# A two-layer convolution attention kernel: image 0's projections in free PSUM banks, and another table of slots

## What is computed

```python
h = _group_norm(x, gn_w, gn_b).reshape(B, C, H * W)
qkv = jnp.einsum('oc,bcn->bon', qkv_w, h) + qkv_b[None, :, None]
q, k, v = jnp.split(qkv, 3, axis=1)
attn = jax.nn.softmax(jnp.einsum('bcn,bcm->bnm', q, k) * scale, axis=-1)
h = jnp.einsum('bcm,bnm->bcn', v, attn)
x = x + (jnp.einsum('oc,bcn->bon', proj_w, h) + proj_b[None, :, None]).reshape(B, C, H, W)
...
q, k, v = (W x + b for (W, b) in ((Wq, bq), (Wk, bk), (Wv, bv)))
attn = jax.nn.softmax(jnp.einsum('bdi,bdj->bij', q, k), axis=-1)
x = gamma[0] * jnp.einsum('bcj,bij->bci', v, attn) + x
```

## Time and profile before

| | |
|---|---|
| median of 3 runs | 1599.27 us (1598.35 to 1600.09) |
| the profiled execution | 1598.83 us |
| its span, first to last instruction | 1597.1 us |
| PE / PEld busy | 1507.5 (94%) / 1095.0 (69%) us |
| DVE / ACT / POOL busy | 1289.0 (81%) / 1205.5 (75%) / 1245.6 (78%) us |
| mean granted TensorE clock | 0.997 |

### The profile page before, as it was taken

One profiled execution on the slowest core, in us unless ns is written; L12 is line 12 of the kernel. 1 busy time (PEld: TensorE's weight loads), 2 busy tenths in 40 slices (PEclk: granted clock), 3 DMA queues, 4 the chain that ended last, 5 costly groups with the idle time before them and its releaser, 6 DMA issues. The chain is left out here.

```text
span 1597.1 us, 43928 instructions
## 1 busy us (share of the span) xinstructions
PE 1507.5 (94%) x16777; PEld 1095.0 (69%) x16777; DVE 1289.0 (81%) x2499; ACT 1205.5 (75%) x1698; POOL 1245.6 (78%) x1036
## 2 busy tenths in 40 slices
PE   4799999999999999999999999999999999999977
PEld 2477777767777767777767777767767767777656
DVE  3678888888888888888888888888888888888875
ACT  1678778777778777778777778777778777778774
POOL 5778888878788888788888788888788888788653
PEclk9999999999999999999999999999999999999999
DMA  1899999999999999999999999999999999999999
GB/s 49 143 167 187 196 196 200 199 195 202 207 190 200 204 202 194 197 195 203 204 195 197 207 186 203 195 208 200 197 195 196 208 195 201 201 193 188 188 188 175
DMA packets 1081439, 305.23 MB, mean 191 GB/s; under 512 B 1068272, under 2 KB 1068944, under 8 KB 1081232
## 3 DMA queue, kind: packets, MB, share of 16 engines
q1 hardware_dynamic: 1080080, 302.41, 107.9%
q10 hardware_dynamic: 1152, 0.00, 0.0%
HBM read 17.13 MB, written 16.78 MB: 21 GB/s over the span
## 5 line engine op out<-in xcount | busy, mean ns | idle before, releaser
L769 PE MATMUL mixed<-v_head,pt 128*128 128x129 f16 x4096 | 714.9, 222 | 0.0
L771 PE MATMUL mixed<-v_head,pt 128*128 128x129 f16 x4096 | 714.7, 219 | 0.0
L770 PE MATMUL mixed<-v_tail,pt 128*128 128x128 f16 x4096 | 714.6, 218 | 0.0
L546 DVE TENSOR_REDUCE nmax<-scores 128x1 f32<-128x1024 f32 x512 | 601.4, 1216 | 46.8 <-PE scores L754 28.5
L353 POOL TENSOR_TENSOR rows<-prob,rows 128x1024 f16<-128x1024 f32 x256 | 545.0, 2129 | 21.4
L447 ACT ACTIVATE scores<-scores,nmax 128x1024 f32<-128x1024 f32 x256 | 278.6, 1088 | 287.5 <-DVE nmax L546 287.5
L348 POOL TENSOR_SCALAR rows<-prob 128x1024 f16<-128x1024 f32 x256 | 267.1, 1043 | 258.9 <-ACT prob L442 257.3
L563 DVE SCALAR_TENSOR_TENSOR rows<-scores,rows 128x1024 f16<-128x1024 f32 x256 | 313.6, 1225 | 137.2 <-ACT rows L455 137.2
L770 PEld LDWEIGHTS mixed<-v_tail,pt 128*128 128x128 f16 x4096 | 404.4, 99 | 2.7
L769 PEld LDWEIGHTS mixed<-v_head,pt 128*128 128x128 f16 x4096 | 397.6, 97 | 0.2
L771 PEld LDWEIGHTS mixed<-v_head,pt 128*128 128x128 f16 x4096 | 395.5, 97 | 0.0
(11 more groups left out here) (91 smaller groups left out, 1843.3 us busy)
## 6 DMA issues: line engine op xcount, KB each, us to landing
x_raw<-in_x_dram SPq DMA_DIRECT2D x32, 512.0 KB, 4.8
out_dram<-y SPq DMA_DIRECT2D x64, 256.0 KB, 2.8
pt<-rows SPq DMA_TRANSPOSE x512, 4.9
w_qkv<-in_L_conv_qkv_w_dram SPq DMA_DIRECT2D x3, 64.0 KB, 3.9
b_qk<-in_L_conv_bk_dram SPq DMA_DIRECT2D x8, 0.1 KB, 2.0
b_qk<-in_L_conv_bq_dram SPq DMA_DIRECT2D x8, 0.1 KB, 1.6
w_proj<-in_L_conv_proj_w_dram SPq DMA_DIRECT2D x1, 64.0 KB, 3.7
w_v<-in_L_conv_Wv_dram SPq DMA_DIRECT2D x1, 64.0 KB, 3.6
```

The lines of the kernel that those rows point to most:

```text
L546: nc.vector.reduce_max(nmax[l][:, tile.i % TILES:tile.i % TILES + 1], scores[l][:, :], AX.X, negate=True).then_inc(maxed[l], 1)
L769: mm(mixed[l][:, 0:C + 1], head, vh[:, p, m, 0:C + 1], start=(m == 0), stop=False)
L770: mm(mixed[l][:, 0:C], head, vt[:, p, m, :], start=False, stop=False)
L771: done = mm(mixed[l][:, 0:C + 1], tail, vh[:, p, m, 0:C + 1], start=False, stop=(m == TILES - 1))
```

## The change

The tables of slots are others, for the first images and for all. `V1_BUFS` gives the layer 1 values a third buffer. Image 0's QK projections go to `bank_w` and to the two halves of `scores[1]` in place of `bank_t`, and its `h_tail` and its q and k splits are made by DVE, not POOL. The weight transposes go to `mixed`, in three set-up pieces at other slots with semaphores of their own, and x of image 1 is loaded before the last four weights and the biases. In short (W's columns are V, qk1 and v1, two halves each; offsets count from `start0(n)`):

```diff
+V1_BUFS = 3
-FIRST_SLOT, SETUP_SLOT = -16, -8
-HEADED, DVE_SETUP, PE_SETUP, SET_UP = -6, -4, -2, -1
+FIRST_SLOT = -16
+
+SETUP_QK, SETUP_V, SETUP_FOLD, SETUP_QK1, SET_UP = -8, -5, -2, 1, 3
+BIASED = -6
...
-LOADS = Steps(-16)
-STATS = Steps(-12, -11)
-GN = Steps(-10, -9)
-ROOT, H_FULL = Steps(-8, first={1: (-7,)}), Steps(-7, first={1: (-6,)})
-H_HEAD, H_TAIL = Steps(-7, first={1: (-6,)}), Steps(-6, first={1: (-5,)})
...
-QK = Steps(-5, -4, -3, 0, first={0: (-5, -4, -3, -2), 1: (-4, -3, -2, -1)})
...
+LOADS = Steps(-21, first={0: (-16,), 1: (-16,), 2: (-16,), 3: (-16,), 4: (-18,)})
+LOADS_LEFT = -11
+STATS = Steps(-19, -16, first={0: (-12, -11), 1: (-11, -11), 2: (-9, -8), 3: (-12, -11), 4: (-16, -16)})
+GN = Steps(-15, -14, first={0: (-10, -9), 1: (-10, -9), 2: (-8, -7), 3: (-10, -9)})
+ROOT = Steps(-13, first={0: (-8,), 1: (-9,), 2: (-6,), 3: (-8,)})
+H_FULL = Steps(-9, first={0: (-7,), 1: (-8,), 2: (-5,), 3: (-7,)})
+H_HEAD = Steps(-11, first={0: (-7,), 1: (-7,), 2: (-5,), 3: (-7,)})
...
+QK = Steps(-5, -4, -3, 0, first={0: (-5, -4, -3, -2), 1: (-4, -3, -2, -1), 2: (-4, -3, -2, 0)})
...
-W = Steps(1, 2, 11, 15, 12, 14,
-          first={n: V_SLOTS.get(n, (1, 2)) + QK1_SLOTS.get(n, (11, 15)) + V1_SLOTS.get(n, (12, 14))
-                 for n in (0, 1, IMAGES - 1)})
...
+W = Steps(-4, 0, 9, 14, 10, 15,
+          first={n: V_SLOTS.get(n, (-4, 0)) + QK1_SLOTS.get(n, (9, 14)) + V1_SLOTS.get(n, (10, 15))
+                 for n in (0, 1, 2, IMAGES - 1)})
...
+        def qk_bank(im, j):
+
+            if im.n == 0 and j in (1, 2):
+                return scores[1][:, (j - 1) * HALF:j * HALF]
+            return bank_t[:, :] if im.n else bank_w[:, :]
...
             load_x(Image(0))
...
+            for j in range(3):
+                sp.dma_start(w_qkv[:, j, :], qkv_w[j * C:(j + 1) * C, :]).then_inc(w_qkv_loaded, 16)
+            load_x(Image(1))
...
+            def qk_split_first(j):
+                s, h = PARTS[j], j % 2
+                part = (slice(None), 0, s, slice(h * HALF, (h + 1) * HALF))
+                dve.wait_ge(qk_out, j + 1)
+                nc.vector.tensor_copy(qk_head[part], qk32[:, s, h, :]).then_inc(qk_headed, 1)
+                dve.wait_ge(qk_headed, j + 1)
+                nc.vector.tensor_tensor(qk_tail[part], qk32[:, s, h, :], qk_head[part],
...
-                bank_t_read()
+                if im.n:
+                    bank_t_read()
+                elif j == 3:
+                    pe.wait_ge(qk_out, 1)
...
-            every_slot(body, FIRST_SLOT, SETUP_SLOT)
+            every_slot(body, FIRST_SLOT, SETUP_QK)
             setup_turns()
-            every_slot(body, SETUP_SLOT, PE_SETUP)
-            setup()
-            every_slot(body, PE_SETUP)
+            every_slot(body, SETUP_QK, SETUP_FOLD)
+            setup_fold()
+            every_slot(body, SETUP_FOLD, SET_UP)
+            pe.wait_ge(setup_dve, DVE_ALL)
+            every_slot(body, SET_UP)
```

More of the change, by code:

```diff
@@ L123 @@
 V, QK1, V1 = (0, 1), (2, 3), (4, 5)
-W = Steps(1, 2, 11, 15, 12, 14,
-          first={n: V_SLOTS.get(n, (1, 2)) + QK1_SLOTS.get(n, (11, 15)) + V1_SLOTS.get(n, (12, 14))
-                 for n in (0, 1, IMAGES - 1)})
-QK1_COPY = Steps(12, 16, first={n: tuple(slot + 1 for slot in QK1_SLOTS[n]) for n in QK1_SLOTS})
+W = Steps(-4, 0, 9, 14, 10, 15,
+          first={n: V_SLOTS.get(n, (-4, 0)) + QK1_SLOTS.get(n, (9, 14)) + V1_SLOTS.get(n, (10, 15))
+                 for n in (0, 1, 2, IMAGES - 1)})
+QK1_COPY = Steps(10, 15, first={n: tuple(slot + 1 for slot in QK1_SLOTS[n]) for n in QK1_SLOTS})
 X1_BIAS = Steps(15, first={0: (9,), IMAGES - 1: (12,)})
@@ L306, in _ @@
             load_x(Image(0))
[L307 to L310, removed]
+            for j in range(3):
+                sp.dma_start(w_qkv[:, j, :], qkv_w[j * C:(j + 1) * C, :]).then_inc(w_qkv_loaded, 16)
+            load_x(Image(1))
+            for dst, src in ((w_proj[:, :], proj_w), (w1_v[:, :], Wv), (w1_qk[0:CQK, :], Wq),
+                             (w1_qk[CQK:2 * CQK, :], Wk)):
                 sp.dma_start(dst, src).then_inc(w_loaded, 16)
@@ L408, in qk_split @@
                 stand_apart()
+                if im.n == 1 and j == 0:
+                    pool.wait_ge(qk_tailed, 4)
+                    stand_apart()
                 nc.gpsimd.tensor_scalar(qk_head[part], qk32[:, s, h, :], 1.0, 1.0, ALU.mult,
@@ new lines, in h_tail_first @@
+            def h_tail_first():
+                dve.wait_ge(h_head_done, 1)
+                dve.wait_ge(h32_done, 1)
+                nc.vector.tensor_tensor(h_tail[:, 0, :], h32[:, :], h_head[:, 0, :],
+                                        ALU.subtract).then_inc(h_tail_done, 1)
+            def qk_split_first(j):
[5 more added lines that the diff above has]
+                nc.vector.tensor_tensor(qk_tail[part], qk32[:, s, h, :], qk_head[part],
+                                        ALU.subtract).then_inc(qk_tailed, 1)
@@ L639, in setup_qk @@
                     dve.wait_ge(setup_dve, 2 * i + 1)
-                    nc.vector.scalar_tensor_tensor(out=w_tail[:, j, :], in0=scores[0][:, j * C:(j + 1) * C],
-                                                   scalar=W_UP, in1=w_head[:, j, :], op0=ALU.mult,
+                    nc.vector.scalar_tensor_tensor(out=w_tail[:, j, :], in0=turned_w, scalar=W_UP,
+                                                   in1=w_head[:, j, :], op0=ALU.mult,
                                                    op1=ALU.subtract).then_inc(setup_dve, 1)
-                dve.wait_ge(setup_loaded, 16 * N_LOADS)
+                dve.wait_ge(b_loaded, 16 * B_LOADS)
@@ L659, in setup @@
                 done.then_inc(setup_dve, 1)
+                dve.wait_ge(consts_made, 8)
                 low, high = ident[:, 0:64], ident[:, 64:128]
@@ L709, in body @@
                     gn_first(im, h)
+                if slot == H_TAIL_FIRST:
+                    h_tail_first()
                 for im, step in GN.at(slot):
                     (gn_second, gn_third)[step](im)
-            every_slot(body, FIRST_SLOT, SETUP_SLOT)
+                for im, j in QK_SPLIT.at(slot):
+                    if im.n == 0:
+                        qk_split_first(j)
+            every_slot(body, FIRST_SLOT, SETUP_QK)
             setup_qk()
-            every_slot(body, SETUP_SLOT, DVE_SETUP)
-            setup()
-            every_slot(body, DVE_SETUP)
+            every_slot(body, SETUP_QK, SETUP_V)
+            setup_v()
+            every_slot(body, SETUP_V, SETUP_FOLD)
+            setup_fold()
+            every_slot(body, SETUP_FOLD, SETUP_QK1)
+            setup_qk1()
+            every_slot(body, SETUP_QK1)
         @block.tensor
@@ L768, in attend @@
                     head, tail = pt[l][:, r, m, :], pt[l][:, r, TILES + m, :]
-                    mm(mixed[l][:, 0:C + 1], head, vh[:, p, m, 0:C + 1], start=(m == 0), stop=False)
-                    mm(mixed[l][:, 0:C], head, vt[:, p, m, :], start=False, stop=False)
-                    done = mm(mixed[l][:, 0:C + 1], tail, vh[:, p, m, 0:C + 1], start=False,
+                    mm(mixed[l][:, 0:C + 1], head, vh[:, b, m, 0:C + 1], start=(m == 0), stop=False)
+                    mm(mixed[l][:, 0:C], head, vt[:, b, m, :], start=False, stop=False)
+                    done = mm(mixed[l][:, 0:C + 1], tail, vh[:, b, m, 0:C + 1], start=False,
                               stop=(m == TILES - 1))
```

134 lines of the change are left out of this document (73 added, 61 removed).

## The result

The changed kernel takes 1611.82 us, median of 6 runs (1610.67 to 1613.06); the kernel before, timed beside it, 1598.81 (6 runs, 1594.99 to 1600.53). The ratio is 1.0084, 95% interval 1.0073 to 1.0095: slower by 13 us. The forecast was 1603.5 in 1592 to 1611: the direction held, the size lies outside the range.

The account below looks back on a forecast made before the run. Each slot was taken as bound by the scores-maximum-exponential ring with DVE's queue, or by PE's own work. Regular periods +6.7, last 16 slots -1.4, image 0 -1.1 make +4.2 on 1598.83; as median 1603.5 us, range 1592 to 1611.

Parts of the forecast that it names:

- The formula for a step: Regular period, one S to the next: the larger of previous slot's D + 4.51 (at least 5.71) and 4.67 + PE's projections.
- D: Time from S to DVE's row maximum of lane 1: about 1.2 with DVE free, longer behind queued work that waits for ScalarE.
- S: Time at which PE starts lane 0's scores in a slot; a slot's step runs from the previous one to its own.
- The start: Image 0: scores at 26.6 instead of 34.48, first exponential some 8.2 us earlier, at 31.6.
- PE's work: Rival: PE's work decides and evening it out pays; period 46.4, some 1558 us, or only 1592; chance 0.13.
- D of slots 0 and 1: Rival that nothing changes: D there comes out 0.1 shorter each, period 48.0 or less, 1597 to 1602 us; chance 0.27.
- The third, a mechanism made larger: Rival: slots 1, 2 and 7 also delay PE's transposes beyond 6.3; period 48.5, 1611 us; chance 0.1.
- step 7: Slot 7 of the regular period: 1.67 + 4.51 = 6.18 us, in a period of 48.13 against 47.88.
- slots 0 to 16: First slots of the program: give back the earlier first exponential, +7.1 us, slot 0 alone +4.1.
- the low clock: Slot 0: nine score products at 1.2 instead of 2.4 GHz cost some 2 us; a third taken, 0.7.
- the set-up of qk1: Slot 0: 1.38 of copies and about 1.0 of small steps on DVE ahead of slot 1's maximum, another 0.9 us.
- the last 16 slots: End of the program: slots 1, 2 and 6 lose their additions; 46.5 and 46.3 against 94.3 for the two, -1.4 us.

Follow-up runs that it names:

- Runs 2: Changed kernel with a slot's statistics issued on DVE ahead of lane 1's fp16 tail: 1603.41 us, 1.0025 of the kernel before.
- run 3: Changed kernel with the group norm step ahead of the bank_w tail on DVE, from slot 16 on: 1601.51 us, 1.0014 of the kernel before.
- Run 4: Changed kernel with PE's wait for the slot's adds ahead of the bank_w projections, not behind them: 1606.81 us, 1.0051 of the kernel before.
- Run 11: Changed kernel with the V projection of image 3's first half in slot 13, not 12: 1611.29 us, 1.0078 of the kernel before.
- run 10: Kernel before, own order; loads from the fourth image on bring 64 of 1024 columns, stores an eighth: 1598.32 us, 0.9993.
- three orders: Statistics ahead of lane 1's tail, group norm step ahead of bank_w tail, adds' wait ahead of projections; on the kernel before: 1594.04 us, 0.9978.

## Why the prediction was right and wrong

**Right.** The formula for a step, the larger of D + 4.51 and 4.67 + PE's extras, gave seven of eight steps within 0.03, and D of slots 0, 1 and 6 within 0.01. Runs 2 and 3 moved D and the next step moved with it: 1.75 to 1.18 and 6.22 to 5.72; 1.75 to 1.34 and 6.26 to 5.86. The attends behind slot 5's scores, put 0.45 late at 2.40 after S, started 2.39 after it (468.31 to 470.70). PE's idle time ahead of S in slots 1, 2 and 7 was 0.35, 0.14 and 0.61, not 0.5 in each. The start came as said, though the prediction's -8.2 does not follow from its own 34.48 and 26.6, which are 7.9 apart; the first exponential came 8.7 earlier (39.8 to 31.1). These rows are PE's first QK product (forecast 14.0), its first score product (26.6), and DVE's h_tail (1.2 to 1.4):

```profile
14.13 0.61 PE L774 MATMUL bank_w<-h_head,w_head 128*128 128x512 f16 x1 [0.92 <-DVE gs L628]
...
26.37 0.63 PE L774 MATMUL scores<-qk_head 128*128 128x512 f16 x1
```
```profile
12.43 1.21 DVE L659 TENSOR_TENSOR h_tail<-h,h_head 128x1024 f16<-128x1024 f32 x1
```

The rivals fall. Steps 1, 2 and 7 are not PE's work, and the period did not go to 46.4; D of slots 0 and 1 did not come out 0.1 shorter. The third, a mechanism made larger, named nearly the measured time, but not its cause: its sign was an attend of slot 2 over 2.6 after S, and it started 2.16 after (444.64 to 446.80), with the period at 48.30 and not 48.5.

**Wrong, step 7: the hand-off after a lone v1 projection (+4.9 us).** The prediction put slot 7 at 1.67 + 4.51 = 6.18 and the period at 48.13. The 4.51 was read from the steps behind slots 4 and 6 of before, where a QK projection or a group norm product stands between the wait for the adds and the scores. Here that wait stands right between v1 and the scores, and PE is 0.2 later. It measured 6.40. Run 4 moved only the wait: 6.19. The prediction had even noted 0.08 of this kind behind a V projection, and did not ask where it comes from. The trace of before already held the full case, in its last 16 slots behind a lone v1 projection: the exponential ends at 1511.05, and the score product starts 0.26 later.

```profile
1509.94 1.11 ACT L442 ACTIVATE prob<-scores,ebias 128x1024 f32<-128x1024 f32 x1
```
```profile
1511.31 0.38 PE L724 MATMUL scores<-qk_head 128*128 128x512 f16 x1 [0.31 <-ACT prob L442]
```

Over 27 periods the 0.22 of step 7 are 5.9; the other seven steps together came 0.05 short (-1.4), and rounding and single longer periods make up the rest of the 4.9.

**Wrong, slots 0 to 16 (+2.6).** Of it 1.8 is slot 12, put at 6.9. That two projections share bank_w there stood in the table (V of image 3, qk1 of image 1), and the forecast added their PE time, but put the wait between them at nothing. PE's, ScalarE's and DVE's rows of that slot:

```profile
119.67 1.08 PE L886 MATMUL bank_w<-x,w_qk_t 128*128 128x512 f32 x2
122.50 0.22 PE L774 MATMUL bank_w<-w_head,h_head 128*128 128x128 f16 x1 [1.75 <-DVE qk L638]
...
123.81 0.38 PE L774 MATMUL scores<-qk_head 128*128 128x512 f16 x1
```
```profile
120.79 0.78 ACT L496 ACTIVATE qk_masked<-bank_w,b_masked,masks 128x512 f16<-128x512 f32 x1
```
```profile
121.60 0.75 DVE L638 SCALAR_TENSOR_TENSOR qk<-bank_w,b_qk,qk_masked 128x512 f16<-128x512 f32 x1 [0.45 <-ACT qk_masked L496]
```

qk1's product ends at 120.75. ScalarE reads the bank only from 120.79, when its exponential is through, DVE's tail follows at 121.60, and PE's V product waits for it until 122.50: 1.75 idle. S follows 3.05 after the exponential's end in place of 0.06. Run 11 moved the pair, and the cost went with it. Another 0.45 is slot 0, which the prediction charged a third of 2 us for the low clock. PE idled for 4.79 us, and the clock was at 0.50, the 1.2 GHz level, for all the products of both lanes:

```profile
36.59 0.55 PE L909 MATMUL bank_t<-mv,group_mean 128*128 128x1 f32 x2 [4.79 <-DVE mv L616]
37.01 0.59 PE L774 MATMUL scores<-qk_head 128*128 128x512 f16 x1
```
```profile
36.90:42.00 5.10, 5.10 (x14) 1.88 (x14) 3.58 (x28) 0.00 (x0) 2.57 (x3) 0.50 1.06 132
```

Lane 1's row maximum that follows, on DVE:

```profile
41.05 2.50 DVE L568 TENSOR_REDUCE nmax<-scores 128x1 f32<-128x1024 f32 x2 [1.03 <-PE scores L776]
```

All nine products ahead of it ran at the low clock, some 2 us longer in sum (one starts 0.43 behind the other, 0.22 in a regular slot). But the 0.9 for the set-up of qk1 did not come on top: DVE was through with it at 40.01 and then waited 1.03 for PE. So the two terms, 0.9 and 0.7, came as about 2.0 together, and slot 0 took 11.17 (forecast 10.7). The trace agrees with what the Trainium skill (TensorE: Matmul & The Clock Gate, Part 1) says of the throttled state as the default. The 4.5 that the prediction names for a certain cold start is not its own sum, which with 2.0 in place of 0.7 is 5.4; slot 0 took 4.55 more than before (11.17 against 6.62), and that this is so near is luck, since the set-up was hidden.

Slots 1 and 2 took 0.55 more than forecast, nearly all of it slot 1 (9.09). Image 2's second group norm product waits there for ScalarE's copy of a QK projection out of bank_t, so that S is 46.47, 1.01 behind the exponential's end at 45.46, where before it was 0.05:

```profile
46.09 0.52 PE L909 MATMUL bank_t<-gs,group_mean 128*128 128x1 f32 x2 [2.85 <-ACT qk L491]
```

The low clock is no news in slot 1: the kernel before has it there too. The slots left over came 0.2 under the forecast.

**Wrong, the last 16 slots (+1.5).** They were to lose the additions to D in slots 1, 2 and 6. They lost them, but the formula had no term for the lone qk1 tails (D 1.48) and for hand-offs of 0.14 and 0.25, and the 16 slots took 94.4 in place of 92.8.

**By chance**, the end gave back 1.2, since one slot at low clock (slot 253, 7.07 us before) took 5.59. It is an accident of the profiled execution: in the other runs this slot takes 5.6 or 7.0 to 7.2, whatever their table (5.59 in run 10, with the kernel before's). The terms sum: -0.5 + 2.6 + 4.9 + 1.5 - 1.2 = 7.3, and 4.2 + 7.3 = 11.5, the difference of the spans. Another 1.0 of the miss lies outside the profiled span: 0.4 around it (2.16 us in place of 1.72), and the median of the runs is 1.0 above the profiled one where the forecast had 0.4.

The range's upper end, 1611, held a period of 48.5 by slips of 0.08 and late norms. The measured 48.30 lay below that; what the range lacked was that the errors of slots 0 to 16, of the period and of the last 16 slots add up.

## What to carry to other kernels

When a schedule is moved by slots, list for every slot what stands on each in-order queue ahead of the one instruction that the ring waits for, and charge the queue and not the sum of the work: here the same work in other slots cost 0.42 us a period, and changing the order within a slot (run 3) gave back as much as moving the slots had lost. Two users of one PSUM bank in a slot cost the readers' whole delay between them on top of their PE time. And before paying for a shorter ring, look at what else has no slack at the new pace: of the 18 to 21 us that three orders should have brought to the kernel before, some 4 came, since loads and stores then made the transposes late.

## What the runs showed of the hardware

**Transposes made late by loads and stores.** A period of 47.17 us holds 16 transposes and 1 MB of loads and stores. In the run with most of those bytes left out every period but one (47.45) took 47.2; with them ScalarE and GpSimd waited 148 us for transposes, at a DMA share of 1.15 and 199 GB/s in the regular stretch (without them 1.08 and 182):

```profile
192.00:1430.00 1238.00, 1204.09 (x13584) 878.60 (x13582) 1037.29 (x1994) 975.53 (x1372) 1006.72 (x830) 1.00 1.15 199
```

The Trainium skill (DMA: Bandwidth & Descriptors, Latency and other measured facts) gives a transpose 261 GB/s in its slower form; no run here reaches that rate, and the writers were already late at 199. The rate alone does not tell: the kernel before moves 199 GB/s too, with 1.3 us of such waits.

**VectorE held up by GpSimd.** In the new start, DVE's smallest operation is one of its longest:

```profile
23.49 1.64 DVE L701 TENSOR_TENSOR gam_bv<-gam,b_v 128x1 f32<-128x1 f32 x1
...
25.50 1.49 DVE L668 TENSOR_TENSOR qk_tail<-qk,qk_head 128x512 f16<-128x512 f32 x1
```
```profile
23.00 2.12 POOL L399 TENSOR_TENSOR h_tail<-h,h_head 128x1024 f16<-128x1024 f32 x1 [2.70 <-ACT h_head L509]
25.10 1.35 POOL L408 TENSOR_SCALAR xb<-x_raw,bias 128x1024 f32<-128x1024 f32 x1
```

The 128x1 operation takes 1.64 us and ends with GpSimd's subtraction (23.00 + 2.12 = 25.12, 25.13 here). V's product, which waits for it, starts at 25.13. The 512-wide subtraction at 25.50 takes 1.49 beside GpSimd's next operation and 0.69 elsewhere. The Trainium skill (SBUF — State Buffer, SBUF: two separate sides) says that GpSimd and a VectorE operation with two inputs in SBUF take a shared port pair by exclusive lock, held for the whole instruction; the trace agrees. No experiment here took the collision away.

**A wait that is passed late costs even when its condition is long met.** The wait for adds that had ended 1.2 us before the projection did, passed late ahead of PE's score product, made the hand-off 0.26 in place of 0.05 us (run 4). How many waits make how much was not taken apart.
